# Graph network with two adjacency products: a ring of in-place weight tiles, and half of the row tiles multiplied as high and low parts

## What is computed

```python
def _L0_gnn_ref(h, adj, W1, W2, b):            # h (4096, 128), adj (4096, 4096), W2 (16, 128, 128)
    node = h @ W1                               # (4096, 16)
    hw = jnp.einsum('nc,kcf->nkf', h, W2)
    x = jnp.einsum('nk,nkf->nf', node, hw)
    x = adj @ x
    x = x + node @ b
    return jax.nn.relu(x)

def _L1_gnn_ref(z, dist_matrix, W, B):
    msg = z @ W + B
    sens = jnp.exp(-(1.0 / dist_matrix - 1.0) ** 2 / (2.0 * 0.5 * 0.5))
    weights = jnp.where(dist_matrix < 1.0, sens, 0.0)
    return weights @ msg

x = _layernorm(x + _L0_gnn_ref(x, adj, L0_gnn_W1, L0_gnn_W2, L0_gnn_b), axis=-1)
x = _layernorm(x + _L1_gnn_ref(x, adj, L1_gnn_W, L1_gnn_B), axis=-1)
```

## Time and profile before

| | |
|---|---|
| Median of the three runs | 616.05 us |
| Profiled execution: its own time | 615.5 us |
| Profiled execution: span from the first to the last instruction | 613.6 us |
| TensorE busy | 586.6 us (96%) |
| VectorE busy | 472.9 us (77%) |
| ScalarE busy | 457.6 us (75%) |
| GpSimd busy | 97.6 us (16%) |
| DMA | 142.11 MB, mean 232 GB/s |

### The profile page before, as it was taken

One profiled execution on the slowest core, in us unless ns is written; L12 is line 12 of the kernel. 1 busy time (PEld: TensorE's weight loads), 2 busy tenths in 40 slices (PEclk: granted clock), 3 DMA queues, 4 the chain that ended last, 5 costly groups with the idle time before them and its releaser, 6 DMA issues.

```text
span 613.6 us, 5662 instructions
## 1 busy us (share of the span) xinstructions
PE 586.6 (96%) x1618; PEld 297.9 (49%) x1618; DVE 472.9 (77%) x541; ACT 457.6 (75%) x500; POOL 97.6 (16%) x75
## 2 busy tenths in 40 slices
PE   5999999998999999999999999999999999997886
PEld 4877777543444444444444444444444444443332
DVE  5999999807277787777777777777777777789994
ACT  2877668934377788778877778787877777889964
POOL 2678788700000000000000000000000000000320
PEclk9999999999999999999999999999999999998999
DMA  7920000387887787777767886787778777345302
GB/s 235 422 103 19 17 0 1 120 294 253 320 316 275 273 327 317 271 283 289 296 272 284 322 321 258 292 314 273 291 278 305 268 289 314 137 141 194 144 34 103
DMA packets 24480, 142.11 MB, mean 232 GB/s; under 512 B 2672, under 2 KB 4880, under 8 KB 8080
## 3 DMA queue, kind: packets, MB, share of 16 engines
q1 hardware_dynamic: 24464, 141.92, 60.0%
HBM read 139.81 MB, written 2.10 MB: 231 GB/s over the span
## 4 chain that ended last, share of the span: by engine, by line
PE 79%; DVE 9%; ACT 6%; issue 4%; DMA 1%; SPq 0%; DVEq 0%; ACTq 0%
PE acc_ps L329 35%; PE l_ps L363 31%; PE hw_ps L309 3%; DVE part_acc L579 3%; PE hw_ps L310 3%; PE hw_ps L311 3%; DVE wts L596 2%; ACT wts L465 2%; ACT wts L470 2%; DVE wts L606 1%; PE acc_ps L338 1%; PE msg_ps L352 1%; ACT wts L476 1%; DMA x_in<-xT_dram 1%; DVE x L583 1%
## 5 line engine op out<-in xcount | busy, mean ns | idle before, releaser
L363 PE MATMUL l_ps<-wts,msg 128*128 128x512 f32 x512 | 232.0, 597 | 6.5 <-DVE msg L630 4.0
L329 PE MATMUL acc_ps<-row_in,x 128*128 128x512 f32 x512 | 229.0, 592 | 0.0
L465 ACT ACTIVATE wts<-col_in 128x2048 f32<-128x2048 f32 x64 | 122.1, 1908 | 87.2 <-PE l_ps L363 75.2
L606 DVE SCALAR_TENSOR_TENSOR wts<-wts 128x2048 f32<-128x2048 f32 x64 | 147.4, 2304 | 40.6 <-ACT wts L470 40.6
L363 PEld LDWEIGHTS l_ps<-wts,msg 128*128 128x128 f32 x512 | 97.4, 191 | 131.4 <-issue 127.2
L329 PEld LDWEIGHTS acc_ps<-row_in,x 128*128 128x128 f32 x512 | 96.7, 190 | 118.7 <-issue 118.6
L596 DVE SCALAR_TENSOR_TENSOR wts<-col_in,wts 128x2048 f32<-128x2048 f32 x64 | 146.8, 2293 | 0.0
L470 ACT ACTIVATE wts<-wts 128x2048 f32<-128x2048 f32 x64 | 122.2, 1909 | 1.8
L476 ACT ACTIVATE wts<-wts 128x2048 f32<-128x2048 f32 x64 | 121.2, 1894 | 0.4 <-DVE wts L606 0.4
L764 POOL TENSOR_TENSOR row_in<-sumT 128x512 f32<-128x512 f32 x5 | 10.3, 2063 | 469.2 <-DVE sumT L706 469.2
L640 DVE TENSOR_TENSOR sumT<-l_ps,sumT 128x512 f32<-128x512 f32 x64 | 44.1, 690 | 52.9 <-PE l_ps L363 52.9
(11 more groups left out here) (52 smaller groups left out, 196.1 us busy)
## 6 DMA issues: line engine op xcount, KB each, us to landing
row_in<-adjT_dram SPq DMA_DIRECT2D x64, 1024.0 KB, 4.8
col_in<-adjT_dram SPq DMA_DIRECT2D x64, 1024.0 KB, 6.7
x_in<-xT_dram SPq DMA_DIRECT2D x8, 256.0 KB, 3.2
x_row<-xT_dram SPq DMA_DIRECT2D x8, 256.0 KB, 6.4
outT_dram<-sumT SPq DMA_DIRECT2D x8, 256.0 KB, 2.0
W_in<-W_dram SPq DMA_DIRECT2D x2, 512.0 KB, 4.5
B_sb<-B_dram SPq DMA_DIRECT2D x1, 256.0 KB, 4.3
W_sb<-W_dram SPq DMA_DIRECT2D x1, 64.0 KB, 3.7
```

Of the source, the lines that this page charges most:

```text
L329: mm = pe.matmul(acc_ps[:, :], x0[:, k, :], row_in[:, g % RING, c, :], start=(g == 0 and c == 0), stop=False)
L363: mm = pe.matmul(l1_ps[:, j % L1_BANKS, :], msg[:, k, :], wts[:, slot, k, :], start=(k == 0), stop=(k == CH - 1))
L465: act.activation(wts[:, slot, :, :], col_in[:, slot, :, :], ACT.Ln, bias=TINY).then_inc(ln_made, 1)
L606: dve.scalar_tensor_tensor(out=w, in0=w, scalar=2.0, in1=w, op0=ALU.subtract, op1=ALU.mult).then_inc(square_made, 1)
```

## The change

- *Weight tiles in place.* One ring of eight tiles `wt` takes the place of `col_in` and `wts`. The mask now comes first (w times (w < 1)), and logarithm, inverse, square and exponential are all written over the same tile. The last two slots lie over memory of the first stage and are loaded after it. TensorE's column tile comes 12 steps after the row tile of its number (`COL_LAG`), while its weights are made at step m + 7 (`exp_step`).
- *Squares.* VectorE takes the square of five blocks out of eight (`DVE_SQUARED`), ScalarE that of the other three.
- *Row tiles.* For the source blocks 1, 3, 5 and 7 (`SPLIT`) VectorE splits the row tile into `adj_hi` and `adj_lo` two steps ahead, and `x0` once into `x0_hi` and `x0_lo`; TensorE multiplies in three passes of float32r per chunk, 12 in place of 4 float32 matmuls. The other four blocks stay as they were.
- *First stage.* One partial sum per chunk, and the last product is written straight to `x0`; x is rounded, and the node product made, in the middle of the block before; W2 comes in quarters, the first one on the queue of ScalarE, like W1.
- *Layer norms.* The mean is subtracted by TensorE (a matmul with I - 1/128, `centre_w`), so VectorE's centring goes; two buffers for `acc_ps`, `x_row` and `msg`; GpSimd squares nothing any more. All loops are unrolled.

```diff
-LAG = 3
-LEAD = 1
-TAIL_LAG = 2
...
+ROW_RING = 4
+WT_RING = 8
+LATE_SLOTS = 2
+COL_LAG = 12
+SPLIT = (1, 3, 5, 7)
+SPLIT_LEAD = 2
+DVE_SQUARED = (1, 3, 5, 6, 7)
...
+    def mask_step(m):
+        return exp_step(m) - 1
+    def exp_step(m):
+        return 2 * m + 1 if m < 6 else m + COL_LAG - 5
...
@@ sync
+            def load_row_tile(i):
+                before = i - ROW_RING
+                if before >= 0 and is_split(before):
+                    sp.wait_ge(adj_lo_made, splits_before(before) + 1)
+                elif before >= 0:
+                    sp.wait_ge(row_tile_done, before + 1)
+                sp.dma_start(row_in[i % ROW_RING][:, :, :], adjT[i // NB, i % NB]).then_inc(row_tile_in[i % ROW_RING], 16)
+            def load_wt(t):
+                at_least(sp, col_tile_done, t - WT_RING + 1)
+                sp.dma_start(wt[t % WT_RING][:, :, :], adjT[t % NB, t // NB]).then_inc(wt_in[t % WT_RING], 16)
...
@@ tensor
+                if is_split(i):
...
+                    pe.wait_ge(adj_lo_made, n + 1)
+                    hi, lo = adj_hi[n % 2], adj_lo[n % 2]
+                    for c in range(CH):
+                        k = SPLIT.index(g) * CH + c
+                        pe.matmul(acc, x0_hi[:, k, :], hi[:, c, :], start=(g == 0 and c == 0), stop=False)
+                        pe.matmul(acc, x0_hi[:, k, :], lo[:, c, :], start=False, stop=False)
+                        mm = pe.matmul(acc, x0_lo[:, k, :], hi[:, c, :], start=False, stop=False)
...
+            for i in range(STEP_COUNT + 2):
+                r, g = i // NB, i % NB
+                if i < TILES:
+                    row_tile(i)
+                    if g == NB - 1:
+                        node_bias(r)
+                if g == 0 and 1 <= r <= NB:
+                    centre(r - 1)
+                if g == 3 and 1 <= r <= NB:
+                    messages(r - 1)
+                t = i - COL_LAG
+                if 0 <= t < TILES:
+                    col_tile(t)
+                if g == 1 and 1 <= r <= NB:
+                    variance(r - 1)
+                j = t - (TILES - NB)
+                if 0 <= j - 1 < NB:
+                    centre2(j - 1)
+                if 0 <= j - 2 < NB:
+                    variance2(j - 2)
...
@@ scalar
+            act.dma_start(W1_sb[:, :], W1).then_inc(w1_in, 16)
+            load_W2(act, 0)
...
+            for i in range(STEP_COUNT + 2):
+                r, g = i // NB, i % NB
+                if g == 1 and 1 <= r <= NB:
+                    square(r - 1)
+                if g == 2 and 1 <= r <= NB:
+                    inverse_root(r - 1)
+                for t in exps_at.get(i, []):
+                    take_ln(t)
+                    take_inverse(t)
+                for t in left:
+                    take_exp(t)
+                left = []
+                for t in exps_at.get(i, []):
+                    if on_dve(t):
+                        left.append(t)
+                    else:
+                        take_square(t)
+                        take_exp(t)
...
@@ vector
-                        acc = part_acc[:, c, k % 2, :]
...
-                    if q == QUARTERS - 1:
-                        dve.wait_ge(sum_step, g * STEPS + c * (K + 1) + K)
-                        dve.tensor_tensor(x0[:, bass.ds(g * CH + c, 1), :], part_acc[:, c, 0:1, :], part_acc[:, c, 1:2, :],
-                                          ALU.add).then_inc(sum_step, 1)
+                            acc = part_acc[:, c, :]
...
+                                out = x0[:, g * CH + c, :] if k == K - 1 else acc
...
+            def split_row_tile(i):
...
+                dve.tensor_copy(flat(hi[:, :, :]), flat(whole[:, :, :])).then_inc(adj_hi_made, 1)
+                dve.wait_ge(adj_hi_made, n + 1)
+                dve.tensor_tensor(flat(lo[:, :, :]), flat(whole[:, :, :]), flat(hi[:, :, :]),
+                                  ALU.subtract).then_inc(adj_lo_made, 1)
...
             for half in range(2):
                 dve.wait_ge(hw_made[half], NB * GROUPS)
+            dve.wait_ge(fold_step, NB * FOLDS)
+            for i in range(SPLIT_LEAD):
+                if is_split(i):
+                    split_row_tile(i)
+            if NB - 1 in SPLIT:
+                split_x0(NB - 1)
             dve.wait_ge(w1b_made, 1)
             dve.tensor_copy(W1b[:, :], w1b_ps).then_inc(w1b_copied, 1)
...
+            for i in range(STEP_COUNT + 4):
+                r, g = i // NB, i % NB
+                if g == 0 and 1 <= r <= NB:
+                    residual(r - 1)
+                if g == 4 and 1 <= r <= NB:
+                    copy_messages(r - 1)
+                if 0 <= i - COL_LAG - 1 < TILES:
+                    add_part(i - COL_LAG - 1)
+                if i + SPLIT_LEAD < TILES and is_split(i + SPLIT_LEAD):
+                    split_row_tile(i + SPLIT_LEAD)
+                for t in masks_at.get(i, []):
+                    mask(t)
+                if g == 2 and 1 <= r <= NB:
+                    scale_row(r - 1)
+                    add_row(r - 1)
+                for t in exps_at.get(i, []):
+                    if on_dve(t):
+                        take_square(t)
```

More of the change, by code:

```diff
@@ L348, in messages @@
             def messages(r):
                 pe.wait_ge(x1_made, r + 1)
+                pe.wait_ge(ln_var_made, r + 1)
                 for c in range(CH):
@@ new lines, in variance2 @@
+            def variance2(j):
+                pe.wait_ge(sq2_made, j + 1)
+                at_least(pe, ln_var2_made, j - 1)
+                pe.matmul(var2_ps[j % 2][:, :], mean_w[:, :], sq[:, j % 2, :], start=True,
+                          stop=True).then_inc(var2_made, 1)
+            pe.wait_ge(w1_in, 16)
+            node_product(0)
+            for g in range(NB):
+                hidden(g)
+            pe.wait_ge(const_in, CONSTS)
+            pe.wait_ge(sum_step, NB * STEPS)
+            pe.wait_ge(prods_made, NB * GROUPS)
@@ L542, in _, with take_ln @@
-            for r in (0, 1):
-                row(r)
-            with act.Fori(2, NB - 1) as r:
-                row(r)
-            row(NB - 1)
-            for g in range(NB + TAIL_LAG + SCALE_LAG):
-                tail(g)
+                    if n == GROUPS - 3 and g + 1 < NB:
+                        copy_node(g + 1)
+            def take_ln(t):
+                w = wt[t % WT_RING]
+                act.wait_ge(mask_made, t + 1)
+                act.activation(w[:, :, :], w[:, :, :], ACT.Ln, bias=TINY).then_inc(ln_made, 1)
```

693 lines of the change are left out of this document (283 added, 410 removed).

## The result

The changed kernel takes 621.04 us (median; 620.79 to 621.25, 4 runs), against 616.23 us for the kernel before on the same chip (615.05 to 617.22): ratio 1.0079, 95% interval 1.0060 to 1.0097. It is slower, by 0.8%. Forecast was 610.7. The profiled span is 619.5 us against 613.6, where the prediction had 608.2.

What follows compares the result with a forecast made beforehand. TensorE was taken to bound the first stage and the steady part. Terms -7.3 (first stage), +15.0 (turn), -24.1 (steady part), +11.0 (tail) gave -5.4 us: span 613.6 to 608.2, median 616.05 to 610.7; 8-in-10 range 603 to 620.

Steps and rivals of the forecast that it cites:

- First stage: T from 111.9 to 104.6: First stage: its end moves from 111.9 to 104.6 us; VectorE's 90 us fall below TensorE's 93.9, so TensorE bounds.
- T: The time at which the first stage ends: 111.9 us before, forecast 104.6.
- T to the first column tile: Turn from the first stage's end to the first column tile: 62.8 us in place of 47.8, through VectorE's longer list.
- From there to E: Steady part, first column tile to last row tile: 354.6 us in place of 378.7, with TensorE still the bound.
- E: The time at which TensorE reaches the last row tile: 538.4 us before, forecast 522.0.
- Rival A: Steady part: the three engines block each other, a row takes 57.5 us instead of 55.8, time 621.7; chance 0.18.
- D: Split row tiles: passes not cheaper, 0.43 us each, 5.2 us a tile against 2.72, time 689 us; chance 0.02.
- After E: Tail after the last row tile: 86.2 us in place of 75.2, last messages after 29 us instead of 21.
- three signs of being wrong: Rows over 56.5 us, TensorE waiting for split tiles in the middle, or a pass over 0.24 us.
- signs of being right: First stage's last pass near 104 us, then VectorE idle 5; first y 43 us later; rows 55.8 us without TensorE gaps.

Runs made afterwards that it cites:

- e5: Changed kernel with the first stage's conversion of x to x_hi made by ScalarE instead of VectorE, from the second block on: 618.21 us.
- e12: Changed kernel with the next block of x rounded after the third quarter of a block instead of the second: 616.77 us.
- e3: Changed kernel with no split row tiles and no splits of x0, all row tiles in float32: 629.68 us.
- e2: Changed kernel with each of GpSimd's fold additions cut to 128 elements, leaving out part of the sum over k: 605.9 us.
- e7: Changed kernel with e5 and e6 together, x_lo made after a block's third quarter, all splits of x0 at step 4 after the folds: 606.27 us.
- e9: Kernel before with GpSimd's fold additions cut to 128 elements, leaving out part of the sum over k: 609.31 us.
- e10: Kernel before without line 583, the last product written straight to x0, leaving out part of the sum over k: 609.11 us.
- e6: Changed kernel with row 0 in float32, last-fold wait and last x0 split at step 4, row tiles 4 to 7 loaded before SyncE's fold wait: 614.79 us.
- e8: e7 with VectorE squaring all of the last eight weight tiles, from number 56 on: 599.17 us.
- e11: e8 with VectorE's addition for the first y moved ahead of the split of row tile 9: 598.75 us.

## Why the prediction was wrong

**The step that failed** is in "First stage: T from 111.9 to 104.6": rounding x was carried over at 8 x (0.4 + 1.55) = 15.6 us, and with it VectorE's sum of 90 us, "less than TensorE's 93.9, so TensorE bounds", which left 3.8 us for waits and slow first passes. At its new place the rounding takes 16.4 + 12.3 = 28.7 us, and the sum is 68.1 for products, 28.7, and 6.9 for three splits of `x0`: 103.7, more than TensorE's. In place of the 3.8 us stand 116.2 - 7.6 - 93.9 = 14.7 (the first pass came at 7.6, forecast 7.0), of which 7 x 1.47 + 0.58 = 10.9 us are TensorE waiting for VectorE. T came to 116.2, +11.6; with the other terms as forecast, 608.2 + 11.6 = 619.8, and 619.5 was measured.

The comparison of the two sums was wrong as a method too, and not only in its numbers. In e5 and e12 VectorE's sum is 89.6 and 90.6 us, the forecast's 90, and T' is still 112.0 and 110.4, with TensorE waiting 5.4 and 4.9 us; in e3 the sum is 99.6, and the stage ends with after. My reading is that a wait at one place of a block is not won back in the rest of it. In the runs the waits are gone at sums of 84.7 (e2) and 75.5 us (e7), where the long pieces of VectorE's work are gone too.

The row that I carried over, 0.42 us for the conversion, was a price at one place: right behind line 583, which had just waited for the fold's first addition (62.79 + 2.40 = 65.19; the conversion starts at 65.26). e12 shows the like at another place: the same instruction a quarter of a block later is 0.44 us. The warning stood in the trace: line 583 took 0.29 us at 18.31, alone, and 1.2 us on average, four times as long for the same 128 elements. The subtraction's 1.55 was such a price as well; where GpSimd is idle it takes 0.69. The prediction knew of this difference, since it priced a split of `x0` at 2.0 us in the stage and at 1.1 "with GpSimd idle", and drew nothing from it for the conversion. I booked the 19.2 us as work that goes. e9 and e10 show that the gain was real but that it was a wait, and a wait says that someone else's instruction sets the price of the neighbours too.

The Trainium skill (SBUF — State Buffer, "Who interferes with whom") describes it: VectorE's copies and conversions in two-port modes, and its instructions with two SBUF inputs against a GpSimd instruction that reads SBUF, contend for a shared port pair that one instruction holds to its end while "the other **fully blocks**". The trace agrees in both directions: conversion 2.50 us beside a fold and 0.42 with GpSimd idle, fold 8.37 us beside masks and 4.49 without, products from PSUM 337 and 340 ns. The prediction didn't weigh it, though the change puts two-port work into the middle of GpSimd's folds.

**T to the first column tile**, 62.8: measured 63.0, with `y` at T + 43.5 (43.3). Conversion and subtraction of a split 1.22 and 2.29 us (1.25 and 2.3). VectorE waited 4.96 us for the fold (5). This price was right, and e6 shows that it could be cut by 6.7 us. The clock fell in both stretches of the turn, to 0.96 and 0.91, which is about 1.7 us each, and the turn was no longer for it, as the prediction had it.

**From there to E**, 354.6: measured 354.5, rows of 55.7 us (55.8), no gap. Rival A, the three engines blocking each other here, didn't happen; its time, 621.7, comes near the result by chance. D is out too: a pass takes 0.23 us.

**After E**, 86.2: measured 85.8, the messages at E + 28.4 (29), and the clock 0.94 and 0.90 in the two stretches of the tail.

So three of four terms were within 0.4 us, and the fourth had the wrong bound, whose range (waits of 0 to 7.6 us) rested on the same carried-over row. Of the three signs of being wrong none came, since all of them watch the steady part; of the signs of being right the first did not come, the last pass near 104 us. A rival "the rounding meets the fold" could have been worked out from line 583: it lost 1.20 - 0.29 = 0.9 us at each meeting, some 7 us for eight conversions. The way would have been right and the size too small; measured were 1.6 us for each conversion.

**What a better version is.** e7, e8 and e11 keep the change, compute all of the reference, and take the converting work out of the way of the folds. e8 and e11, at 599, are 2.7 and 2.9% under the kernel before.

## What to carry to other kernels

When the same instruction on the same shape takes four times as long in one place as in another, it may be waiting inside its busy time, as line 583 did: find who runs beside it, here GpSimd, before its duration is used as a price anywhere. An engine's sum over a stage being below the other's doesn't make the other the bound: with 90 us on VectorE against 93.9 on TensorE, e5 and e12 still lost 5 us to waits. Work of VectorE that converts or reads two tiles from SBUF belongs into the gaps of GpSimd, onto ScalarE, or behind the stage; one number that says after which quarter it stands was worth 4.3 us. And a wait that is taken from an engine's list mustn't be put into a queue ahead of loads that don't need it.
